# A macaron block (routed experts, attention, routed experts) with its router matmuls turned round into four column strips and its logits transposed on VectorE

## What is computed

```python
def ffn(tokens, router_w, router_b, expert_weights):       # 8 experts, top 2
    logits = einsum('bsh,eh->bse', tokens, router_w) + router_b
    probs = softmax(logits); top_p, top_i = top_k(probs, 2)
    w = top_p / (sum(top_p) + 1e-10)
    y_all = einsum('nh,ehd->ned', x, expert_weights)
    return sum over the two chosen experts of w * y_all     # scaled by factors near 1
x = x + 0.5 * ffn(layernorm(x), ...)
x = x + attention(layernorm(x), ...)      # causal, 8 heads, 2 latent key-value heads of 32
x = x + 0.5 * ffn(layernorm(x), ...)
```

## Time and profile before

| | |
|---|---|
| median of three runs | 512.28 us (512.12 to 513.83) |
| the profiled execution | 512.54 us |
| its span, first to last instruction | 510.8 us |
| PE busy | 462.2 us (90%), 3166 matmuls |
| DVE busy | 415.8 us (81%) |
| ACT busy | 336.8 us (66%) |
| POOL busy | 302.2 us (59%) |
| chain that ended last, by engine | PE 70%, DVE 14%, ACT 6%, issue 5%, POOL 2%, DMA 2% |

### The profile page before, as it was taken

How to read it: one execution, slowest core, us unless ns; L and a number is a source line. 1 busy time by engine, 2 the same in 40 slices (tenths; PEclk the granted TensorE clock), 3 DMA queues, 4 the chain that set the end, 5 groups by cost and what they waited for, 6 DMA issues and landing times.

```text
span 510.8 us, 9871 instructions
## 1 busy us (share of the span) xinstructions
PE 462.2 (90%) x3166; PEld 251.1 (49%) x3166; DVE 415.8 (81%) x1320; ACT 336.8 (66%) x748; POOL 302.2 (59%) x323
## 2 busy tenths in 40 slices
PE   1896989998699999999999999999999999899752
PEld 1673535453254446464645664555534545454441
DVE  6787789989976988989969999988888877863454
ACT  3356417667359767797787976677776496788523
POOL 4166006209745940598489737298498129889835
PEclk9995967999889999999999999999999999999967
DMA  7001310002001010002110100210101000000000
GB/s 199 16 22 42 88 48 22 1 2 81 19 2 32 18 33 2 1 1 58 23 57 13 53 1 2 48 33 17 53 2 54 1 1 2 1 23 1 22 21 21
DMA packets 21123, 14.50 MB, mean 28 GB/s; under 512 B 2952, under 2 KB 20944, under 8 KB 21072
## 3 DMA queue, kind: packets, MB, share of 16 engines
q1 hardware_dynamic: 21072, 13.88, 10.6%
HBM read 3.78 MB, written 2.10 MB: 11 GB/s over the span
## 4 chain that ended last, share of the span: by engine, by line
PE 70%; DVE 14%; ACT 6%; issue 5%; POOL 2%; DMA 2%; SPq 1%; ACTq 0%; POOLq 0%; DVEq 0%
PE bank L1257 12%; PE bank L1235 11%; PE bank L1212 11%; PE bank L1165 6%; PE bank L1262 5%; PE bank L1166 5%; PE bank L1167 5%; DVE diff L861 3%; PE bank L1240 2%; PE bank L1183 2%; ACT prob L739 2%; ACT xn L675 2%; PE bank L1279 2%; DMA x<-in_L_attn_x 2%; PE bank L1152 1%
## 5 line engine op out<-in xcount | busy, mean ns | idle before, releaser
L739 ACT ACTIVATE prob<-bank,exp_scale 128x512 f32<-128x512 f32 x288 | 188.6, 690 | 61.2 <-PE bank L1240 33.1
L620 POOL TENSOR_TENSOR sums<-sums,prob 128x1024 f32<-128x1024 f32 x48 | 112.3, 2371 | 9.5 <-ACT prob L739 9.5
L1212 PE MATMUL bank<-k_stack,q_stack 96*128 96x512 f16 (+3 forms) x384 | 101.2, 336 | 8.5 <-DVE m_part L963 5.4
L1235 PE MATMUL bank<-q_stack,k_stack 98*128 98x512 f16 (+3 forms) x384 | 105.3, 330 | 2.0 <-ACT prob L739 1.5
L704 ACT ACTIVATE scaled<-bank,gate 128x128 f32<-128x128 f32 x256 | 75.3, 374 | 28.7 <-POOL x L598 10.5
L591 POOL TENSOR_TENSOR pair_sum<-dve_sum,scaled 128x256 f32<-128x256 f32 x64 | 46.7, 730 | 80.2 <-DVE dve_sum L947 66.7
L967 DVE TENSOR_REDUCE m_part<-bank 128x1 f32<-128x512 f32 x128 | 83.4, 679 | 7.0 <-PE bank L1212 6.4
L963 DVE CUSTOM_DVE_ANT_0 masked<-bank,mask_qk 128x384 f32<-128x384 f32 (+1 forms) x128 | 75.1, 617 | 8.5 <-PE bank L1212 8.3
L1257 PE MATMUL bank<-prob,v_lat 128*32 128x512 f32 (+3 forms) x768 | 81.8, 500 | 0.1
L1165 PE MATMUL bank<-we_hi,xT_hi 128*128 128x512 f32 x128 | 66.8, 522 | 1.6 <-DVE m_part L963 1.6
L1235 PEld LDWEIGHTS bank<-q_stack,k_stack 98*128 98x128 f16 x384 | 33.4, 98 | 64.7 <-ACT prob L739 32.0
(11 more groups left out here) (128 smaller groups left out, 722.8 us busy)
## 6 DMA issues: line engine op xcount, KB each, us to landing
q_stack<-q_hi SPq DMA_DIRECT2D x32, 128.0 KB, 3.2
x<-in_L_attn_x SPq DMA_DIRECT2D x8, 256.0 KB, 3.0
q_stack<-q_lo SPq DMA_DIRECT2D x16, 128.0 KB, 3.2
out_x<-x SPq DMA_DIRECT2D x8, 256.0 KB, 2.3
k_stack<-k_hi SPq DMA_DIRECT2D x16, 64.0 KB, 2.1
we<-in_L_ffn_expert_weights SPq DMA_DIRECT2D x1, 512.0 KB, 4.0
x<-in_L_attn_wq SPq DMA_DIRECT2D x1, 512.0 KB, 6.6
x<-in_L_attn_wo SPq DMA_DIRECT2D x1, 512.0 KB, 7.9
```

Of the source, the lines that this page charges most:

```text
L620: nc.gpsimd.tensor_tensor(into, first if j == 1 else into, new, ALU.add).then_inc(sum_step, 1)
L739: nc.scalar.activation(prob[:, n % NP, :], bank[ST + n % NST][:], ACT.Exp, scale=exp_scale[:, 0:1]).then_inc(p_ready, 1)
L1212: last = mm(into[:, n * w:(n + 1) * w], q_stack[0:MROW, c, g * NR + r, (i % TC) * P:(i % TC + 1) * P], k_stack[0:MROW, b % 2, g, k:k + w], ...
L1235: last = mm(into[:, at:at + CH - off], k_stack[:, b % 2, g, j * P:(j + 1) * P], q_stack[:, c, g * NR + r, off:CH], start=at == 0, stop=not ...
```

## The change

The router's two operands change places. The weights are now the router's matrix alone, as a plain fp32 tile `rwT` of 128x32 whose last 24 columns are zero, and the tokens are moved. The tokens of a tile are split by `r` into four runs of 32; run `r` of all four tiles (128 columns) goes into the strip of partitions 32r to 32r+31 of the logits' bank, so the experts lie on the partitions. That is done for `xT_hi` and for `xT_lo`, both read as plain fp32: 8 matmuls a chunk again. Step 0 of `routing` becomes a transposition of 32x32 blocks from PSUM into a new SBUF tile `g_t`, which puts each token back on its partition; step 1 adds the bias `rb_sb` to it and writes PSUM. The low part of the router's matrix, with its subtraction on DVE and the wait for it, is gone; a memset of `rwT` is new.

```diff
-        rw_parts = sb("rw_parts", [P, 2 * NE], F32R)
+        rwT = sb("rwT", [P, DL])
...
+        g_t = sb("g_t", [P, NT, DL])
...
-            logits = home[:, 0:2 * nt * NE].rearrange("p (t e) -> p t e", t=nt)
+            logits = home[:, 0:nt * DL]
...
+                act.wait_ge(set_up, NE + 4)
+                copy(rwT[:, 0:NE], bank[0][:, 2 * DL:2 * DL + NE]).then_inc(prep_act, 1)
...
+            V.memset(rwT[:], 0.0).then_inc(set_up, 1)
...
-                if i == 0:
-                    dve.wait_ge(prep_act, 2)
-                    V.tensor_tensor(rw_parts[:, NE:2 * NE], bank[0][:, 2 * DL:2 * DL + NE], rw_parts[:, 0:NE].bitcast(F32),
-                                    ALU.subtract).then_inc(low_split, 1)
...
-                step(0, None, V.tensor_tensor, s_1, logits[:, :, 0:NE], bias_b, ALU.add)
-                step(1, 0, V.tensor_tensor, p_l, logits[:, :, NE:2 * NE], s_1, ALU.add)
+                step(0, None, V.transpose, g_t[:, 0:nt].rearrange("p t e -> p (t e)"), logits)
+                step(1, 0, V.tensor_tensor, p_l, g_t[:, 0:nt, 0:NE], bias_b, ALU.add)
...
-                for t in range(TC):
-                    hi, lo = x_parts(2 * f, n, t)
-                    k = (n - u.n) * TC + t
-                    into = logits[:, k * 2 * NE:(k + 1) * 2 * NE]
-                    mm(into, hi, rw_parts[:], start=k == 0, stop=False, skip_group_check=True)
-                    last = mm(into[:, 0:NE], lo, rw_parts[:, 0:NE], start=False, stop=k == u.count * TC - 1,
-                              skip_group_check=True)
+                at = slice((n - u.n) * P, (n - u.n + 1) * P)
+                hi, lo = (part[:, xt_home(2 * f, n), :].bitcast(F32).rearrange("p (t r i) -> p t r i", r=NR, i=DL)
+                          for part in (xT_hi, xT_lo))
+                for x, first in ((hi, True), (lo, False)):
+                    for r in range(NR):
+                        last = mm(logits[r * DL:(r + 1) * DL, at], rwT[:], x[:, :, r, :],
+                                  start=first, stop=not first, skip_group_check=True)
```

All five order strings are also new; the steps in them are the same ones, save the one subtraction that is gone. The first line of PE's, before and after:

```diff
-    "X2PPX3L6Y7L2Y5Y3Y6PY7PY3Y5Y1Y6Y7Y3UY2Y5UY1Y6Y7x0Q3W2K5X1Q6x7L0Y2Q3W5M1M6M7M5K3M1M6M7M5M1M6X7M5M1M6LM7M5M1Q3M"
+    "X2PPX3L6Y7PL2Y5Y3Y6PY7Y3Y1Y5Y6Y7Y3Y2Y1UY5Y6UY7x3Q2K1W5X0Q6x7L3Y2Q1M5M0W7M6M5M1K7M0X6Q5M1M0M7LM6M1M0Y7M6M1M0M"
```

More of the change, by code:

```diff
@@ new lines @@
+    "6M1M0R6M1M0Y6Y1M5Y0M3M5SM3Y5Y6R7SSM7M1SSM7Y0Y1SM7M5SM6SM7SM5SY6Y0M1Y7M6SV5M1M0M6VSSVM7VM1M0M6M7SM5SM1M0SM6Sx"
+    "7M5SM1SV0M7M6M5SM1VM7M6M5VR1VM7Y6M5M1M0Y7M5Y6SM1SY0K5M6M1SSQ7Q6M1SVSJ5SJSM0JSM1SM7M6VSSM0M1M7M6SJM0SVM1SM7SM"
+    "6M0SM1SM7SM6VSM0M1SM7M6SW5X0VR1M7M5SM6M0SSY7SV5VVSSx1SM6SL0K5SM1SM6VW1X6SSQ5M1SLSQ6SR1SVSY5SM6SVSSM1M6SVSSY1"
+    "SY6VY0SM7SM5M1SM6SM7Y5SSV1SM6M7M5R0VSSM6M7M5SM0VM6M7SSM5V0M1SSM6M7M5VSM1SM6M7M5M1SM6SM7VSM5M1SM6SM7VSJ5SM1M6"
+    "JSM7SM0JM1JY6Y7R0V1VY5SVVSSM6M0Y7M5M1SY6Y0SY5z1SM7SVM7Sz1l7Y6SJ0lVSJSY1JJSx5M6SSM0K1VQ5M6W0SSM1Y6SM0M1SVSM7S"
@@ new lines @@
+    "M5M0M1SM7SVSY5SM0M1Q7SM6SM5M0M1M6V7VVY5M0X1R6Y7Y5Y0x6Y7M1SSM0Y5M6SY1M0M7SY6M5M0SY7SVL1SM6M5SM0R7Y6K5VSSY0M7S"
+    "X6SM5SM7Q0Y5SM7LVSSQ6W0M5SM7M0SY6M5Y7Y0SSM5VSVM7SR5SM6M0SM7M5SM6SY0SSY7SM5SY6Y1SM5Y0M7M6SY5SSM7M6M1Y0SY7SM5Y"
+    "6Y1V5SSM0M7M6VVSSM1M0M7M6SY5SM1SY0J7M6JJJSM5M1M6M0V7VVVSM5M1Y6SM0Y7Y5M1Y6M7V5VVR0VM6x1M7M0z6Q5M1z7M0SM1M6SK5"
+    "SM0l7lJ1SJM6SSM5VJSSQ0JM6VSx5SM1SW6M5M1SSM6Y5SM1VSSY6M0M1Y7SVSM0M5M6M7SM1SY0SVR5SSY6SY7SY0M1SV5VVM1SM6SM7Y0S"
+    "M5Y1Q6Y7SM1SK0M5SM7SY1Q5M7SY0Y1M6M7VM0Y5M1SM6Y7SVM0M1M6SSM5M7Y0SSR1VM6SSM5M0M7SM1SM6M5SSM0M7VSSM1M6VSSM5M0SM"
@@ new lines @@
+    "CCCxCPCxCCPCPxnnnnnnnCCCxCCCCCXPPPXXXCxCCCxxnnnnnnnQXXKXXNNNNNNNIQMQMMMMMKIMMMMMGMMGMGGGMGGGGMGGGGMGMGGRGGMG"
+    "GQMGGGGGGGMMCMCCCMCCCRCCMMxMCCCxCCMMxMCCMCCCCMMxCnnMCCCnnnXnXnxXXMxMMMDMMMMMMMMDDMMMMMMBMMMRDMMMMMDMCCCCCMMC"
+    "DCKCMQQxMxMnnMMnnXMnnMMMMMMMMMXMMJMMBMMnXXNNNIMNNMRMMNzNzzzDDDMMMKIMGGGQGGGGQGRGMGGGGGGMMGGGGGGGGGGGGCCCCCCC"
+    "CMMMMMCxCCCxMMMRMMMMxDMMMDDMMMMMMMMMMMMMMMDMMMMDBMDJCCRCCzzzzmmmmmmmxnnnnnnnDMMMMDDCCCCCMixMCCCiCCCGGGGCGGGG"
+    "GGGGJzzGzGzGMxGMKGxGGGMGGGGGGMGQMMCCCMMMMMCMMMQxnnnnnnMnMMMDBCCCCMDRDICCCCMMCCCCMMMCCCCMMCCCCMMMRKCMCCCMMIQM"
@@ new lines @@
+    "GGGGGGGGGGQMMMMCGCGGGGGMGCCGCCCGCMRGMMGMMGGGMGGGCMCCCCCMMMCCCxMCCCMCMMCCCCCCCxxxnMnMnMnnnnDMDDMMMMCMCCCJzzzz"
+    "mmmMmmmMmxMMxDBDDMMCCCCMCCCCMMxxnnnnnnnRMDMDMDMiQMiMMKGMMMGGGGGGGGGGGJGGMGGGGGMGzzGMMMQGGzzGMGGGCMCCCMMMMMCB"
+    "CCCMRMCCCCDMDMDMCCCCMCCCCMMMKQMCCCCQMMMMMCCCCMMMMCCCCMRMMMMMMMMMMMMMMMMMRMMMMMMDDDMMMMMMMMMMMBMMMJzzzzmmmmmm"
+    "mMRMDDDMMMMMMMMMiMMiMMGMDDDGGGGGGGGGGGGGMGGGGGGGGGGGGGCMCCMCBCJCCCzzzzmmmmmmmRCCCCDDDCCCCiCCCCCGGGGGGGGGCGCC"
+    "GGGGGGGGGGGGGGGGCGCCCCCCCDDDCCCCCCCCJzzzzmmmmmmmCCCCCCCCiGGGGGGGGGGGGGGGGGGGGGGGGGGGCCCCCCCCCCCCCCCC"
@@ L221 @@
+    "CCCEQEEnnOnnXRCCCCCCCCxNENECCCCNEECCCCNEEEERCCCCKEEEXEEQCCCCEEEQLWEECCCEECEEREEEEEEECCCCCCCCEEECCCCEECECECCC"
+    "CCCEEOEEECCECnCnnnEEOEmCCECCmCCCCmmmmmmROxnnznnQzEEKEEEElEEQExEEWEEEEECCCCCCCCEEEEEREEEEECCCCCCCCOEEECCCCQEE"
+    "KEECCCCEQCCCCEECCCCEEEREEEEEEEEEEEEEREEEEEOWEEEEEEEEEEREOEmmmmEmmmEmEEEzEEEEzEEEEOEEElEEEECECCCCCECCEEEEEERE"
+    "mmmmCCCCOCCCEECzECCECCECECECCECElCECCEEEEEEECCCCEEEEEEEEECCOCCCCCCCCCCCCCCmmmmzlCCCCCCCCCCCCCCCC"
 )
 POOL_ORDER = (
-    "NNNNNNFFFFFFFFFFFFFFFFnnFFFFFFFFnnNNFFFFFFFFFFFFFFFFFFnnYFFFFFFYAAAAAAAAnnNNYAAAAAAAFFFFAFFFFFYYFFFmmnnFFFYA"
@@ L449, in route_bank @@
             nt = u.count * TC
-            logits = home[:, 0:2 * nt * NE].rearrange("p (t e) -> p t e", t=nt)
-            part = [home[:, i * NT * NE:i * NT * NE + nt * NE].rearrange("p (t e) -> p t e", t=nt)
-                    for i in range(2, 6)]
-            small = [home[:, 6 * NT * NE + i * NT:6 * NT * NE + i * NT + nt] for i in range(2)]
+            logits = home[:, 0:nt * DL]
+            part = [home[:, i * NT * NE:i * NT * NE + nt * NE].rearrange("p (t e) -> p t e", t=nt) for i in range(4)]
+            small = [home[:, 4 * NT * NE + i * NT:4 * NT * NE + i * NT + nt] for i in range(2)]
             return logits, part, small
@@ L1017, in _ @@
             merges, den_steps = (Q for Q in range(NB * NQ) if QUADS[Q % NQ][0]), product(range(NB * NQ), range(3))
-            weight_parts, low_parts = iter(range(2)), [product([l], range(NN)) for l in (0, 2)]
+            low_parts = [product([l], range(NN)) for l in (0, 2)]
             for step in DVE_ORDER:
@@ L1044, in _ @@
                 elif step == "H":
-                    low_weights(next(weight_parts))
+                    low_weights()
                 elif step in "Ii":
```

58 lines of the change are left out of this document (16 added, 42 removed).

## The result

The changed kernel takes 504.88 us (median of four runs, 504.49 to 506.44) where the kernel before took 512.2 us (510.23 to 513.83) beside it: ratio 0.9868, 95% interval 0.9822 to 0.9915, 1.3% faster. The prediction was 508.6 us within 503.5 to 515.5 us, faster with a chance of 0.55. The profiled execution took 504.58 us, its span is 502.8 us (510.8 before). Runs over 1.5% above the fastest of their kernel stand in the medians but not in the ratios, so a ratio can differ a little from the quotient of two medians.

A forecast was written before the change was run, and what follows sets the result against it. The prediction took PE to bound from 145 to 430 us, after a DVE-bound stage; 3.95 + 0.2 + 1.1 off and 0.2 + 0.7 + 0.7 on made 3.65 us off, 508.6 us at the median, range 503.5 to 515.5 us.

The forecast's parts named there:

- What bounds: By stage: DVE bounds from 117 to 145 us, PE from 145 to 430 us, PE and POOL together to 478 us.
- A warm chunk, 0.56 us: Router on PE, 145 to 430 us: 0.56 us a chunk; ten chunks fall from 9.55 to 5.6 us, 3.95 us off.
- the entry into strips: PE's change from full width into strips at each router chunk: no row for its price, taken as nothing.
- Rival B: Strips don't pay on PE (drain at each change, or 32-column runs at half pace): 515.4 or about 512.5 us; chance 0.06.
- The eleventh chunk, 0.2 us: Router chunk near 456 us, where POOL bounds as well: saves 0.4 us, half counted, 0.2 us off.
- Head and tail, 1.1 us: Both ends, PE cold, first gate step waits for the router: net 0.56 us off at either end, 1.1 us off.
- DVE's transposition, 330 and 458 ns: Step 0 of the gates on DVE: about 330 ns for one chunk, 458 ns for two; 0.2 us on.
- Step 1, 0.7 us: DVE's addition of two SBUF operands waits behind POOL's sums: DVE loses about 4.6 us, 0.7 us on.
- Rival C: Step 1 runs into POOL's sums; if 8 us of DVE's waits reach PE, 516 us; chance 0.15.
- The products ahead of the last quad, 0.7 us: On PE, three expert products now ahead of the last quad's last two groups, where before they filled a wait: 0.7 us on.
- The re-plan of the DVE-bound stage, nothing: New order of small statistics against POOL's sums: could give or take 5.4 us of PE's waits; taken as nothing.
- rival D: The re-plan clears the DVE-bound stage: up to 5.4 us less, 503 to 506 us, PE's waits there near nothing; chance 0.17.

The follow-up runs named there:

- E2: The kernel before, old router, with the new order strings and its subtraction put back: 508.06 us, ratio 0.9928.
- E1: The changed kernel, new router, with the order strings of before, less the one subtraction that is gone: 511.52 us, ratio 0.9997.
- E6: E3 with the router's round of `xT_hi` made twice in every router: 506.57 us, ratio 0.9918.
- E7: The kernel before with POOL's sums of the first sequence cut into two additions of 128x512: 509.05 us, ratio 0.9963.
- E3: The changed kernel with the transposition written into the free half of the logits' PSUM bank, `g_t` gone: 502.83 us, ratio 0.9825; again 502.26 us, 0.9846.
- E9: E3 with the half tile of expert products moved back behind the last two groups of the last quad on PE: 502.19 us, ratio 0.9847.
- E5: E1 with the transposition written into the free half of the logits' PSUM bank: 509.13 us, ratio 0.995.
- E8: E3 with POOL's sums of the first sequence cut into two additions of 128x512: 502.12 us, ratio 0.9841.

## Why the prediction came out as it did

By stage, in us; the form is E2 to the changed kernel (in brackets before to E1), the order before to E2 (in brackets E1 to the changed kernel):

| | forecast | measured | form | order |
|---|---|---|---|---|
| head | -0.6 | -4.6 | -3.5 (-2.8) | -1.1 (-1.8) |
| DVE-bound stage | +0.2 | -3.1 | -0.1 (-0.3) | -3.0 (-2.8) |
| PE-bound stage | -2.8 | +0.4 | -0.3 (+1.5) | +0.7 (-1.1) |
| tail | -0.6 | -0.7 | -0.6 (-0.5) | -0.1 (-0.2) |

**What bounds.** The reading held: PE bounds the long stage (E6), DVE the one before it (E2, E7).

**A warm chunk, 0.56 us: right, but its saving, 0.4 us, was mis-sized.** The new chunk takes 0.55 to 0.58 us where full width follows, 0.46 where strips follow. The runs of 32 columns cost nothing. What was wrong is that both chunks were priced from their own first start. Two chunks in the same place, between two scores, in E2 and in the changed kernel:

```profile
450.20 0.39 PE L1235 MATMUL bank<-q_stack,k_stack 98*128 98x512 f16 x1
450.25 0.36 PE L1152 MATMUL bank<-rw_parts,xT_hi 128*128 128x16 f32 x1
...
451.25 0.39 PE L1235 MATMUL bank<-q_stack,k_stack 98*128 98x512 f16 x1
```

```profile
446.37 0.39 PE L1232 MATMUL bank<-q_stack,k_stack 98*128 98x512 f16 x1
446.69 0.43 PE L1150 MATMUL bank<-xT_hi,rwT 128*32 128x128 f32 x8
...
447.27 0.39 PE L1232 MATMUL bank<-q_stack,k_stack 98*128 98x512 f16 x1
```

From its own start the router falls from 1.00 to 0.58 us; from score to score, 1.05 becomes 0.90. A score of 512 columns is followed by the next score after 0.22 to 0.23 us. The old router started well before that, 0.05 us behind the score here and 0.03 to 0.12 in most places, so part of the score's time had been counted as the router's. The new one starts 0.31 to 0.32 us behind the score: that is the entry into strips, 0.09 us, which was taken as nothing (nine scores ahead of weighted values in the trace of before show the same 0.31). Over the eleven chunks, from E2 to E3, the routers take 4.6 us less in that stage and the instructions ahead of them 1.7 us more (3.3 for 1.6 us). Net that is 2.8 us, and the stage is 2.7 us shorter, not 3.95 + 0.2. Rival B's drain at each change didn't come: in and out together cost 0.21 us, where it needed 0.80.

**The eleventh chunk, 0.2 us:** not separated; an eleventh of the 2.8 us above is 0.25 us.

**Head and tail, 1.1 us.** The wait from router to DVE shrank by 0.63 and 0.75 us, the net per end was 0.3 to 0.5 (at nearly equal clock) and 0.5 to 0.6 us: right. Of the rest of the head's 4.6 us the order has 0.6 to 1.8 us and the shorter time at the lower clock (33.6 for 51.0 us) what is left, 2.3 us or more; no term had either.

**DVE's transposition, 330 and 458 ns: right**, 0.30 to 0.32 us and 0.44 to 0.45 us.

**Step 1, 0.7 us: mis-sized.** DVE's loss was put at 4.6 us and is 4.8 (5.49 us less four times 0.22, and 0.19 in the fifth unit); but 2.5 us of it reached the end, not 0.7. The row that I had leant on, a PE busy throughout 345 to 378 us, was one wait in one place; the four waits stand elsewhere, and behind three of them PE waits for `q_lo` or a gate. Rival C had this mechanism and fell short of its point: 2.5 of the 8 us that it needed. The Trainium skill (SBUF — State Buffer, Who interferes with whom) says that a DVE instruction with at most one SBUF input, outside its two-port modes, doesn't contend with GpSimd. E3 agrees: 0.23 us at step 1 while a sum ran, 1.52 us with two SBUF inputs.

**The products ahead of the last quad, 0.7 us: mis-sized**, 0.2 to 0.3 us net (E9). I had priced the front of the quad and taken what they filled behind it as free; 0.5 us of it was not.

**The re-plan of the DVE-bound stage, nothing: this is the step that failed.** It gave 3.0 us in that stage, by rival D's mechanism, and 504.9 us lies within D's 503 to 506; with it came the 0.6 to 1.8 us of the head, which D hadn't named. But D's own sign, PE's waits there near nothing, didn't come (3.6 of 5.4 us are left), and the head and the misses in the PE-bound stage had a part in where the time came out. That DVE's waits set the length of this stage is shown in the old order (E7: 3.1 us less of waits, some 2 us less of stage); under the new order it is argued from the same rows. The trace had the rows that price it: 9.7 us of waits behind POOL's sums, and 5.4 us that PE waited. What I lacked was a way to tell from the order alone where the statistics would fall, and I gave it a chance of 0.17.

Added up, the form was forecast at 5.25 us less 0.9 us of costs, and gave between nothing (E1) and 3.4 us (E2 to the changed kernel) by the medians. The order was forecast at 0.7 us on, and gave 3.5 us off under the old router (E2) and 6.9 us off under the new one (E1 to the changed kernel, 511.52 to 504.64). So the two don't simply add. In the PE-bound stage the order costs 0.7 us under the old router, as much as the three products moved into it, and gives 1.1 us under the new one, in both pairs (E1 to the changed kernel, E5 to E3); no run here separates what in the new order does that. The form was forecast too high and the order the wrong way, and the two errors are opposite: that the time lies in the range is in part luck.

## What to carry to other kernels

A gain in one instruction's form must be paid for at the places where its operands now lie: moving a tile from PSUM to SBUF cost 2.5 us through DVE's waits for POOL, nearly all of the 2.7 us that the faster matmuls gave in that stage, and one edit took it back. Price a group of matmuls from the start of the instruction ahead of it to the start of the one behind it: from its own start, the old router looked up to 0.2 us dearer than it was and the new one 0.1 us cheaper. When a change comes with a new order, price the order by itself, from the stage in which two engines share something: the waits that show there are what an order can give or take. And where TensorE's granted clock differs between two profiles, compare stages at equal clock before giving their difference to an edit.

## What I had not expected of the hardware

- Changing between full width and strips of 32 costs PE 0.09 us on the way in and 0.11 to 0.12 us on the way out; the starts show no longer pause.
- A DVE operation with small SBUF operands waits behind a running POOL addition even with one tensor operand, as `neg_mean` at 134.19 and `diff` at 122.89 do; the reductions and transpositions from SBUF between them (in the changed kernel 0.16 us for `neg_mean<-stats` at 118.97 and 0.71 us for `r_t<-rec` at 419.44, both while POOL added) do not.
- Cutting POOL's additions in two costs POOL 2 x 1.27 us for 2.37 (7%, not the 17% that E8's expectation names), and DVE doesn't always get its turn between the halves. In E8 a merge waited through two boundaries, 2.90 us in all:

```profile
133.97 1.27 POOL L624 TENSOR_TENSOR sums<-sums,prob 128x512 f32<-128x512 f32 x1
134.83 2.90 DVE L971 TENSOR_TENSOR m_fin<-m_part 128x16 f32<-128x16 f32 x1
135.20 1.27 POOL L622 TENSOR_TENSOR sums<-sums,prob 128x512 f32<-128x512 f32 x1
136.44 1.26 POOL L624 TENSOR_TENSOR sums<-sums,prob 128x512 f32<-128x512 f32 x1
```
